# Attention scores as plain float32 matmuls on row halves of the array, in place of stacked float32r matmuls

## The reference, cut to what matters

```python
normed = x * jax.lax.rsqrt(jnp.mean(x * x, axis=-1, keepdims=True) + EPS)
qkv = normed @ W_qkv.T + b_qkv
qkv = qkv.reshape(*qkv.shape[:-1], N_HEADS, D_HEAD, 3)
q, k, v = (qkv[..., 0], qkv[..., 1], qkv[..., 2])
scores = jnp.einsum('bqhd,bkhd->bhqk', q, k)
scores = jnp.where(causal_mask, -jnp.inf, scores)
attn = jax.nn.softmax(scores, axis=-2)
z = jnp.einsum('bhqk,bkhd->bqhd', attn, v)
...
```

## Time and profile before

| | us |
|---|---|
| three runs, median | 1500.27 |
| three runs, lowest and highest | 1495.83, 1503.83 |
| span of the profiled execution | 1498.5 |

### The profile page before, as it was taken

One profiled execution on the slowest core, in us unless ns is written; L12 is line 12 of the kernel. 1 busy time (PEld: TensorE's weight loads), 2 busy tenths in 40 slices (PEclk: granted clock), 3 DMA queues, 4 the chain that ended last, 5 costly groups with the idle time before them and its releaser, 6 DMA issues.

```text
span 1498.5 us, 23566 instructions
## 1 busy us (share of the span) xinstructions
PE 1317.3 (88%) x6488; PEld 913.9 (61%) x6488; DVE 892.5 (60%) x2486; ACT 596.9 (40%) x1387; POOL 327.7 (22%) x487
## 2 busy tenths in 40 slices
PE   2699998999999999999999999999998846999996
PEld 0455555556566566565666666666664735888885
DVE  4466666666666766666666665666556561444443
ACT  1255555554544544454544444444444001111110
POOL 2121121112222322222222212121211341111111
PEclk7799999999999999999999999999999967999998
DMA  5656667545666656656655555565557882566540
GB/s 187 168 146 159 170 172 198 144 109 141 149 152 151 160 149 155 152 149 157 160 144 137 140 134 141 133 152 147 149 145 233 307 274 79 187 212 226 177 150 16
DMA packets 146223, 240.21 MB, mean 160 GB/s; under 512 B 15993, under 2 KB 77307, under 8 KB 145913
## 3 DMA queue, kind: packets, MB, share of 16 engines
q1 hardware_dynamic: 137608, 214.50, 53.9%
q10 hardware_dynamic: 4464, 16.25, 2.7%
q0 software_dynamic: 4096, 8.82, 1.6%
HBM read 94.76 MB, written 48.00 MB: 95 GB/s over the span
## 4 chain that ended last, share of the span: by engine, by line
PE 57%; SPq 12%; issue 10%; DVE 10%; DMA 6%; ACT 3%; POOL 1%; DVEq 0%; ACTq 0%; POOLq 0%
PE SC L661 12%; PE Z L673 8%; PE Z L821 8%; PE SC L795 8%; SPq L474 6%; PE XB L636 6%; PE XA L697 6%; PE XA L636 5%; DMA xp<-in_x 4%; DVE SC L1056 3%; ACT E L856 3%; PE XA L646 2%; PE XB L646 2%; SPq L531 1%; DVE nm L1056 1%
## 5 line engine op out<-in xcount | busy, mean ns | idle before, releaser
L1056 DVE CUSTOM_DVE_ANT_0 SC<-SC,mask 128x512 f32<-128x512 f32 (+7 forms) x512 | 380.0, 780 | 259.7 <-PE SC L661 259.4
L856 ACT ACTIVATE E<-SC,nm 128x512 f32<-128x512 f32 (+7 forms) x512 | 376.6, 739 | 380.6 <-DVE nm L1056 380.4
L661 PE MATMUL SC<-QS,KS 128*128 128x512 f32 (+3 forms) x1536 | 352.4, 366 | 19.9 <-DMA KS<-XK 14.0
L673 PE MATMUL Z<-E,vs 128*64 128x512 f32 (+3 forms) x1536 | 304.7, 503 | 59.0 <-DVE vs L1044 59.0
L661 PEld LDWEIGHTS SC<-QS,KS 128*128 128x128 f32 x1536 | 257.1, 196 | 98.4 <-issue 46.0
L673 PEld LDWEIGHTS Z<-E,vs 128*64 128x64 f32 x1536 | 85.4, 136 | 164.1 <-issue 78.4
L821 PE MATMUL Z<-W,hh 128*128 128x256 f32 x512 | 114.9, 383 | 2.2 <-DVE yb L1278 2.2
L795 PE MATMUL SC<-bT,W 128*128 128x256 f32 x512 | 115.0, 384 | 0.0
L1044 DVE TENSOR_TENSOR vs<-V,ri 128x128 f32<-128x128 f32 x256 | 92.7, 362 | 27.3 <-DVE ri L1038 1.1
L795 PEld LDWEIGHTS SC<-bT,W 128*128 128x128 f32 x512 | 98.7, 193 | 13.8
L821 PEld LDWEIGHTS Z<-W,hh 128*128 128x128 f32 x512 | 97.2, 192 | 15.6 <-DVE yb L1278 2.6
(11 more groups left out here) (193 smaller groups left out, 1782.9 us busy)
## 6 DMA issues: line engine op xcount, KB each, us to landing
KS<-XK SPq DMA_DIRECT2D x256, 256.0 KB, 4.6
QS<-XQ SPq DMA_DIRECT2D x128, 256.0 KB, 4.3
W<-in_w SPq DMA_DIRECT2D x32, 1024.0 KB, 8.5
z_s<-zs ACTq DMA_DIRECT2D x31, 512.0 KB, 4.0
zt<-z_s SPq DMA_DIRECT2D x24, 512.0 KB, 4.3
W<-in_wqk SPq DMA_DIRECT2D x33, 257.0 KB, 4.4
slots_s<-zt SPq DMA_DIRECT2D x16, 520.0 KB, 5.8
xb<-slots_s SPq DMA_DIRECT2D x16, 520.0 KB, 3.8
```

The lines of the kernel that those rows point to most:

```text
L661: last = pe.matmul(SC[h][:, at:at + z - a], KS[:, ap, h, part, lo:lo + P], QS[:, ap, h, a:z], start=(part == 0), stop=(part == 1))
L673: last = pe.matmul(Z[DH * h:DH * h + DH, a:z], vs[:, kb % 2, DH * h:DH * h + DH], E[:, h, kb % 2, a:z], start=(kb == 0), stop=(kb == (3 if ...
L856: act.activation(E[:, h, kb % 2, lo:S], SC[h][:, at:at + S - lo], ACT.Exp, bias=nm[:, h, kb:kb + 1], scale=-1.0, accum_out=rs[:, kb, h:h + ...
L1056: dve.tensor_tensor_reduce(SC[h][:, at:at + S - lo], SC[h][:, at:at + S - lo], mask[:, 0:S - lo], 1.0, BIG, ALU.add, ALU.min, nm[:, h, kb: ...
```

## The change

q and k are evacuated once, by ACT, as float32 and with their bias, into XQ and XK, which now have two parities in place of two parts. DVE's second evacuation, SP's 12 copies of each step, QS, KS and the semaphore qk_in are gone. The bank is free when ACT has evacuated. A score of head h is one plain float32 matmul over the 64 rows in which the projection left that head: rows 0 to 63 for head 0, rows 64 to 127 for head 1, 128 columns of weights each. The two heads take turns piece by piece, and the first matmul of a block waits for the exponentials of both heads. A tile without use keeps the memory layout behind it large enough for the experts.

```diff
-        QS = sb("QS", [P, 2, 2, S], F32R, stack=att)
-        KS = sb("KS", [P, 2, 2, 2, S], F32R, stack=att)
-        XQ = sb("XQ", [P, 2, S], F32R, stack=att)
-        XK = sb("XK", [P, 2, S], F32R, stack=att)
+        XQ = sb("XQ", [P, 2, S], stack=att)
+        XK = sb("XK", [P, 2, S], stack=att)
+        sb("room_for_experts", [P, 12 * S], stack=att)
...
-                if st.has("proj"):
-                    sp.wait_ge(scores_done[1], st.n("scores"))
-                    settle(sp, sp_passed)
-                    stack(st, "q", 1)
-                    stack(st, "k", 0)
...
-                    stack(st, "k", 1)
...
-                def score(kb, h):
-
-                    pe.wait_ge(exp_done[h], st.of("expd", kb if kb <= 4 else kb - 1))
-                    if kb == 0:
-                        pe.wait_ge(qk_in[ap], qk_count(st))
+                def score(kb):
+
+                    for h in range(2):
+                        pe.wait_ge(exp_done[h], st.of("expd", kb if kb <= 4 else kb - 1))
                     lo = kb * P
                     spans = [(lo, HALF), (HALF, S)] if lo < HALF else [(lo, S)]
-                    for a, z in spans:
+                    for n, (a, z) in enumerate(spans):
                         at = a if kb < 4 else a - HALF + (kb % 2) * HALF
-                        for part in range(2):
-                            last = pe.matmul(SC[h][:, at:at + z - a], KS[:, ap, h, part, lo:lo + P],
-                                             QS[:, ap, h, a:z], start=(part == 0), stop=(part == 1))
-                    last.then_inc(scores_done[h], 1)
+                        for h in range(2):
+                            rows = slice(DH * h, DH * h + DH)
+                            last = pe.matmul(SC[h][:, at:at + z - a], XK[rows, ap, lo:lo + P], XQ[rows, ap, a:z],
+                                             start=True, stop=True)
+                            if n == len(spans) - 1:
+                                last.then_inc(scores_done[h], 1)
...
-
-                            act.wait_ge(qk_in[1 - pp], qk_count(st))
                         x, k = (XQ, 0) if kind == "q" else (XK, 1)
-                        act.activation(x[:, 0, half * HALF:(half + 1) * HALF], bank[:, :], ACT.Identity,
-                                       bias=qkb[:, pp, k:k + 1], scale=-1.0 if k else 1.0).then_inc(s["hi"], 1)
+                        act.activation(x[:, pp, half * HALF:(half + 1) * HALF], bank[:, :], ACT.Identity,
+                                       bias=qkb[:, pp, k:k + 1],
+                                       scale=-1.0 if k else 1.0).then_inc(auxb_free if half == 0 else auxa_free, 1)
...
-                            dve.wait_ge(s["hi"], st.of("hi", order.index((kind, half)) + 1))
-                            if kind == "q":
-                                last = dve.scalar_tensor_tensor(XQ[:, 1, cols], bank[:, :], qkb[:, pp, 0:1],
-                                                                XQ[:, 0, cols].bitcast(F32), ALU.add, ALU.subtract)
```

More of the change, by code:

```diff
@@ L354, in adaln_block @@
         wv_split = sem("wv_split")
-        qk_in = [sem(f"qk_in{k}") for k in range(2)]
         xln_in = [sem(f"xln_in{k}") for k in range(2)]
@@ L456, in _ @@
             sp.dma_start(woT[:, :, :], wo_d).then_inc(wo_in, 16)
[L458 to L464, removed]
-                    settle(sp, sp_passed)
-                cols = slice(0, S) if kind == "q" else slice(half * HALF, (half + 1) * HALF)
-                for h in range(2):
-                    rows = slice(DH * h, DH * h + DH)
-                    for part in range(2):
-                        to = slice(DH * part, DH * part + DH)
-                        if kind == "q":
[L472 to L475, removed]
             def load_tail(st):
@@ L686, in step @@
                     if st.has("att"):
-                        score(kb, 0)
-                        score(kb, 1)
+                        score(kb)
                         if kb >= 1:
@@ L831, in _ @@
         def _(act):
-            start_counters(act, [*exp_done, auxb_free, s["zevac"], s["hi"], s["ss"], s["hThi"]])
+            start_counters(act, [*exp_done, auxb_free, s["zevac"], s["ss"], s["hThi"]])
             act.wait_ge(mod_in, 48)
@@ L1062, in step @@
                     for kind, half in PIECES[pp].get(kb - 1, ()) if st.has("proj") else ():
+                        if kind != "v":
+                            continue
                         use = piece_use(pp, (kind, half))
-                        cols = slice(half * HALF, (half + 1) * HALF)
                         bank, free, full, at_ = ((XB, auxb_free, auxb_full, st.of("auxb", use)) if half % 2 == 0 else
                                                  (XA, auxa_free, auxa_full, st.of("auxa", st.has("post") + use)))
-                        if kind == "v":
-                            dve.wait_ge(full, at_)
-                            last = dve.tensor_tensor(V[:, 2 * half:2 * half + 2, :, :].rearrange("p t a d -> p t (a d)"),
-                                                     bank[:, :].rearrange("p (t d) -> p t d", t=2),
-                                                     bvB[:, bass.ds(st.j * CV, CV)].unsqueeze(1).broadcast_to([P, 2, CV]), ALU.add)
-                        else:
-                            order = [p for k in sorted(PIECES[pp]) for p in PIECES[pp][k] if p[0] != "v"]
-                            dve.wait_ge(s["hi"], st.of("hi", order.index((kind, half)) + 1))
-                            if kind == "q":
-                                last = dve.scalar_tensor_tensor(XQ[:, 1, cols], bank[:, :], qkb[:, pp, 0:1],
-                                                                XQ[:, 0, cols].bitcast(F32), ALU.add, ALU.subtract)
-                            else:
-                                last = dve.scalar_tensor_tensor(XK[:, 1, cols], bank[:, :], qkb[:, pp, 1:2],
-                                                                XK[:, 0, cols].bitcast(F32), ALU.subtract, ALU.subtract,
-                                                                reverse0=True)
-                        last.then_inc(free, 1)
+                        dve.wait_ge(full, at_)
+                        dve.tensor_tensor(V[:, 2 * half:2 * half + 2, :, :].rearrange("p t a d -> p t (a d)"),
+                                          bank[:, :].rearrange("p (t d) -> p t d", t=2),
+                                          bvB[:, bass.ds(st.j * CV, CV)].unsqueeze(1).broadcast_to([P, 2, CV]),
+                                          ALU.add).then_inc(free, 1)
                     if st.has("ln"):
```

7 lines of the change are left out of this document (1 added, 6 removed).

## The result

The changed kernel takes 1532.63 us in the median of four runs (1524.01, 1524.18, 1541.08, 1542.35), the kernel before 1499.0 beside it. The ratio is 1.022, with a 95% interval of 1.017 to 1.028: slower, by about 2%. The profiled run took 1524.01 us with a span of 1522.3, so its trace can explain +23.8 us of span against the 1498.5 of the earlier trace rows. The runs at 1541 are taken up under the clock.

A forecast was written before the change was run, and what follows sets the result against it. It took PE, busy for 88% of the span, as the bound. Its terms 11 + 14 + 22 + 9 + 3 - 26 = +33 us on the 1498.5 us span gave 1531.5 profiled and 1533 us median, range 1480 to 1600.

The forecast's parts named there:

- What goes: First step's wait for KS with its low clock, and most KS and xp waits on PE, disappear: -26 us.
- PE's own work for the scores: Score blocks on PE save nothing, and entering the new shape costs what follows 0.3 to 0.4 us a step: +11 us.
- The wait of block 1: In 9 steps without post, block 1's scores wait for both heads' exponentials: 1.6 us a step, +14 us.
- The waits of blocks 2 to 4: PE waits for exponentials by 0.4, 0.24 and 0.08 us in successive blocks: 0.7 a step, +22 us over 31 steps.
- Block 2, all steps: Before block 2, a chain of 3.77 us from reduction to exponential against 3.37 of PE cover: a 0.4 us wait.
- Blocks 4 to 7: DVE and ACT chain starts 0.5 us later, partly offset by an evacuation that goes: 0.3 us taken, +9 us.
- the 11 for the shape: The +11 us over 32 steps for PE's score work and what follows a score block in the row shape.
- the three waits above: Waits for both heads at block 1 (+14 us), from block 2 on (+22 us) and in blocks 4 to 7 (+9 us).
- The clock, 0: Low clock at step starts: perhaps +14 us from new waits and -12 from missing ones, taken as 0.
- Missing overlap: Rival: row halves don't overlap, so score blocks cost 7.7 us more a step, about 1775 us; chance 0.13.
- The free entry: Rival: entering the row shape costs 0.05 us in place of 0.23, 50 us go in all, 1483 us; chance 0.14.
- One more stretch of low clock in each step without post: Rival: chains matter more, each such step drops to low clock once more, tail 0.5 us, 1553 us; chance 0.13.

The follow-up runs named there:

- the bias first: Changed kernel with DVE adding the output projection's bias ahead of block 1's reductions in steps with post; 1524.8 us, ratio 1.020 to the kernel before.
- the coupled kernel: Kernel before with only the new score order: heads alternate piece by piece and a block waits for both exponentials; 1528.3 us, ratio 1.021.

## Why the prediction was right, and where it was not

It said 1533 us, slower. The median is 1532.6. The mechanism that it gave, both heads held to the end of a block on a chain that was only just covered, is the one that the traces show; one of its steps, the clock and the price of the last blocks were off. Point by point:

- **What goes.** Right but for 1.6 us. Attention began at 55.0, 11.5 us earlier for the 10.3 that were said; the 1.6 us for low clock in the first step did not come, since a stretch falls into that step again (it takes 35.9 us, 1.4 more than its like). KS and xp wait no more. The reason given for xp fell with the copies put back: they return, and it doesn't.
- **PE's own work for the scores.** The size of a score block was right: 1.92, 1.70 and 1.49 us for blocks 0, 1 and 2 from start to start (260.80 to 262.72, 266.84 to 268.54, and 1.49 in the step with post), each 0.213 for 128 columns plus 0.21, where the sum took 0.23. The first projection matmul behind block 0 took 0.34 to the next, where it took 0.23 before (260.73 to 260.96). The Trainium skill (TensorEngine Tiling (Array Packing), Key Properties) says that a change of the tiling mode drains the engine; these 0.11 us more agree. The fixed 0.21 of a block tells nothing on it: in the kernel before, block 2's scores follow a 128-row projection without a change of mode and have 0.23 too (1.51 for 6 x 0.213). One gain was not foreseen: block 3's scores took 1.28 us where they took 1.47.
- **The wait of block 1** in steps without post: right. 2.45 us measured for 2.5, and its weighing starts 7.74 us into the step (268.54 - 260.80) where it was 6.17: 1.57 for 1.6.
- **The waits of blocks 2 to 4, +22 us.** The sum was nearly right, for a wrong reason in the steps with post. Block 2 loses 0.34 us to the exponential for the 0.4 that was said. In the 22 steps with post the later reductions push DVE's bias addition behind the point where PE needs bank A, 0.87 us each, 19.0. From block 1 to block 2 such a step takes 6.10 us where it took 5.21, and with the bias first 5.45: of the 0.89 us the bias made 0.65 and the chain 0.24. The step that failed is "Block 2, all steps": it followed the chain of reduction and exponential and not what else is queued behind the reductions on DVE.
- **Blocks 4 to 7.** Too small. From block 4's scores to the step's end the steps take 12.5 us for 12.1 before (even, without post), 13.0 for 12.2 (odd, without), 12.6 for 12.0 (even, with) and 13.2 for 12.7 (odd, with). That is 17 us in all, where 9 were put on the chain and about half of the 11 for the shape falls into these blocks. The reduction of block 4 starts 0.5 us later, as was said; the last weighings wait for it (71.6 us in place of 59.0). The part that was put on the freed evacuation, 0.2 a step, measures 0.25 in every second step.
- **The split between coupling and row shape** can't be settled by the coupled kernel. It costs 27 to 30 us, where the three waits above had 45. The steps come to 44 with 14 given back by KS and xp, so 28 to 31 us are left, where +11 stood for the row shape. But most of what is left isn't the price of the shape, whose entries and exits are as small as said. It is the rest of the coupling, which needs the row halves: since they overlap, both heads end their block together, and the first reduction starts 2.18 us into block 0 and not 1.86, and 1.32 into block 4 and not 0.82. With that the wait before block 1 grows from 2.19 to 2.45, and that for the bias from 0.40 (9.0 us in the coupled kernel) to 0.87. The kernel with the heads in turn is the other half of the test: row halves with the old order and separate waits keep 38 of the 44 us. How many us the shape costs by itself stays open; no kernel was built in which the halves overlap and head 0 still ends its block first.
- **The clock, 0.** Wrong for each run taken alone. The profiled run at 1524 had 10 us less from it. No profile fell on a run at 1541. Its mean granted clock is 0.956 for 0.966, which is 31 us more of low clock, nine stretches; at 1.1 to 1.6 us each they would bring the 1524 to 1534 to 1538, so most of the difference but not all. The median comes out at the forecast since two runs lay on either side of it, and that is luck.
- **Rivals.** Missing overlap is out (1.92 us, not 3.5). The free entry is out (0.21, above the break-even at 0.12). One more stretch of low clock in each step without post did not come either: two of the nine have one.

## What to carry to other kernels

When two streams are tied to one wait, go through everything queued behind the late instruction on the other engines, not only the chain that feeds the wait: here a 0.4 us addition, one place too late on DVE, cost 0.65 us a step where the chain cost 0.24 in the same place. Streams that overlap also end together, and what waited for the first of them starts later, even when the program keeps their waits apart. Before giving up independence for overlap, try whether the engine overlaps the streams in their old order. And compare steps in which the clock is the same: a kernel edit of 14 us disappeared in the total and was plain in the steps.

## What the hardware showed that I had not expected

- Matmuls on different row halves overlap although one head's four come before the other's in the program, and with a separate wait between them (block 1 of the in-turn kernel). With six in a row they overlap in part: 2.25 us for 1.65.
- Three float32r matmuls on row halves are cheaper than one plain float32 matmul: 1.65 us a block 0 for 1.99.
- Low clock came in stretches of 3.4 us, most at the cost of 1.1 to 1.6 us. With the bias first they lay 71.7 us apart over hundreds of us, in step with pairs of steps that took 70.4 us without one and 71.8 with one. An edit on DVE and a shift of the steps both changed their number.
